# Splitting the token-shift transfer of the last stage into one of 112 rows and one of 15

## The reference, cut to what matters

```python
def shift_tokens(t):
    a, s = jnp.split(t, 2, -1)
    s = jnp.pad(s, ((0, 0), (1, 0), (0, 0)))[:, :-1]
    return jnp.concatenate([a, s], -1)

def ffn_layer(x, g, bln, W1, b1, W2, b2):
    mu = x.mean(-1, keepdims=True)
    var = ((x - mu) ** 2).mean(-1, keepdims=True)
    xn = (x - mu) / jnp.sqrt(var + 1e-05) * g + bln
    hg = xn @ W1 + b1
    a, gate = jnp.split(hg, 2, -1)
    return a * jax.nn.gelu(gate, approximate=False) @ W2 + b2

for i in range(DEPTH):                      # DEPTH = 6
    x = attn_layer(shift_tokens(x), Wqkv[i], q_scale[i], k_scale[i], Wo[i]) + x
    x = ffn_layer(shift_tokens(x), ln_g[i], ln_b[i], W1[i], b1[i], W2[i], b2[i]) + x
```

## Time and profile before

| | us |
|---|---|
| median of 3 runs | 4162.72 |
| lowest and highest of them | 4159.46, 4164.74 |
| the profiled execution, its own time | 4165.06 |
| its span, first to last instruction | 4163.3 |
| its mean granted TensorE clock | 0.974 |

### The profile page before, as it was taken

One profiled execution on the slowest core, in us unless ns is written; L12 is line 12 of the kernel. 1 busy time (PEld: TensorE's weight loads), 2 busy tenths in 40 slices (PEclk: granted clock), 3 DMA queues, 4 the chain that ended last, 5 costly groups with the idle time before them and its releaser, 6 DMA issues.

```text
span 4163.3 us, 97842 instructions
## 1 busy us (share of the span) xinstructions
PE 3871.8 (93%) x36632; PEld 2544.0 (61%) x36632; DVE 2904.2 (70%) x10275; ACT 2580.5 (62%) x6856; POOL 1243.2 (30%) x810
## 2 busy tenths in 40 slices
PE   8979578899988999999999999999999999999996
PEld 5668445566655666666666666666666666666664
DVE  3542357788868887777777777777777777777773
ACT  2213246667766767677776676777766766767662
POOL 1103300000005433343434434333434343434330
PEclk9979789999999999999999999999999999999998
DMA  6002210000011001111011101010011101111010
GB/s 181 23 21 73 66 60 2 7 19 22 9 42 29 22 22 48 32 32 27 18 49 30 43 17 53 26 36 24 23 48 32 37 22 38 33 40 29 17 37 18
DMA packets 110785, 146.33 MB, mean 35 GB/s; under 512 B 35748, under 2 KB 77200, under 8 KB 109936
## 3 DMA queue, kind: packets, MB, share of 16 engines
q1 hardware_dynamic: 106912, 130.76, 10.9%
q0 software_dynamic: 3408, 9.31, 0.9%
HBM read 78.31 MB, written 11.40 MB: 22 GB/s over the span
## 4 chain that ended last, share of the span: by engine, by line
PE 54%; DVE 9%; POOL 4%; issue 2%; DMA 1%; ACT 0%; SPq 0%; DVEq 0%; POOLq 0%
PE psum L489 17%; PE psum L586 9%; PE psum L469 7%; PE psum L570 6%; PE psum L603 5%; PE psum L549 4%; PE psum L523 4%; POOL f_rn L892 3%; DVE f_rot L710 2%; DVE f_prob L753 1%; DVE f_rot L712 1%; DVE f_ss L717 1%; DVE f_xn L807 1%; PE psum L592 1%; DVE f_prob L781 1%
## 5 line engine op out<-in xcount | busy, mean ns | idle before, releaser
L489 PE MATMUL psum<-f_wqkv,f_xsT 128*128 128x512 f32 x2304 | 1072.1, 595 | 4.3 <-ACT f_raw L636 2.6
L887 POOL TENSOR_TENSOR f_raw<-f_rot 128x512 f32<-128x512 f32 x384 | 488.7, 1273 | 1663.8 <-DVE f_rot L712 1663.8
L650 ACT ACTIVATE f_prob<-f_prob,f_nb,f_rq 128x128 f32<-128x128 f32 x1536 | 740.1, 487 | 38.6 <-DVE f_nb L766 37.7
L489 PEld LDWEIGHTS psum<-f_wqkv,f_xsT 128*128 128x128 f32 x2304 | 402.5, 191 | 334.2 <-issue 329.4
L892 POOL TENSOR_TENSOR f_rn<-f_ss,f_half_pow 128x32 f32<-128x32 f32 x96 | 524.4, 5463 | 11.2
L586 PE MATMUL psum<-f_xnT,f_w 128*128 128x512 f32 x960 | 437.9, 595 | 2.2 <-ACT f_hT L673 1.1
L753 DVE CUSTOM_DVE_ANT_0 f_prob<-psum,f_band 128x128 f32<-128x128 f32 x1536 | 352.8, 285 | 115.9 <-PE psum L523 114.7
L634 ACT ACTIVATE f_sq<-psum 128x512 f32<-128x512 f32 x384 | 227.8, 593 | 231.1 <-PE psum L489 231.0
L781 DVE TENSOR_SCALAR f_prob<-f_prob,f_rs 128x128 f32<-128x128 f32 x1536 | 341.2, 286 | 13.6
L570 PE MATMUL psum<-f_wo,f_oT 128*128 128x256 f32 x1536 | 347.4, 379 | 1.6 <-ACT f_v L636 0.9
L710 DVE TENSOR_TENSOR f_rot<-f_raw,f_tab 128x512 f32<-128x512 f32 x384 | 333.4, 868 | 14.3 <-DMA x_before_mlp<-x_all 14.3
(11 more groups left out here) (248 smaller groups left out, 6978.3 us busy)
## 6 DMA issues: line engine op xcount, KB each, us to landing
f_v_near<-f_v SPq DMA_DIRECT2D x168, 256.0 KB, 3.5
f_wqkv<-in_Wqkv SPq DMA_DIRECT2D x36, 512.0 KB, 5.8
w_moe_W<-in_L_ffn_W SPq DMA_DIRECT2D x2, 4096.0 KB, 22.4
f_w<-in_W SPq DMA_DIRECT2D x12, 640.0 KB
f_wo<-in_Wo SPq DMA_DIRECT2D x6, 1024.0 KB, 6.4
f_xs<-x_all SPq DMA_DIRECT2D x24, 254.0 KB
expert_rows<-m_y SPq DMA_DIRECT2D x39, 128.0 KB, 1.7
h_mask_int<-in_mask_BxSxS_ik SPq DMA_DIRECT2D x16, 256.0 KB, 2.6
```

The lines of the kernel that those rows point to most:

```text
L489: mm = nc.tensor.matmul(ps.ap(step), xsT[:, c, t * P:(t + 1) * P], wqkv[:, c, i * HALF:(i + 1) * HALF], start=c == 0, stop=c == KC - 1)
L650: ex = nc.scalar.activation(pr, pr, ACT.Exp, bias=nb[:, t % 2, h:h + 1], scale=rq8[:, t, h:h + 1], accum_out=sums[:, t % 2, h:h + 1])
L887: nc.gpsimd.tensor_tensor(raw[:, (4 * t + i) % 8, :], rot[:, n % 2, 0, :], rot[:, n % 2, 1, :], ALU.add).then_inc(rope_done, 1)
```

## The change

Partition rows 1 to 127 of `xs` are no longer filled by one transfer. `EVEN` is (128 - 1) // 16 * 16 = 112: one transfer fills partitions 1 to 112, a second one partitions 113 to 127. The transfer for partition 0 stays. Three transfers now count on `xs_ready` in each body, so VectorE waits for 48 per iteration in place of 32. Nothing else changes.

```diff
--- before.py
+++ after.py
@@ -175,6 +175,7 @@
     H, DH = 16, 64
     WINDOW = W = 64
     R = 32
+    EVEN = (P - 1) // 16 * 16
     TB = 4
     NB = x_all.shape[1] // TB
     KC = D // P
@@ -391,7 +392,8 @@
 
                 at = (b - 1) % NB * TB
                 wait_drained(sp, ps, ("wo", -1, TB - 1), it)
-                sp.dma_start(xs[1:P, :, :], x_all[0:P - 1, at:at + TB, P:D]).then_inc(xs_ready, 16)
+                sp.dma_start(xs[1:EVEN + 1, :, :], x_all[0:EVEN, at:at + TB, P:D]).then_inc(xs_ready, 16)
+                sp.dma_start(xs[EVEN + 1:P, :, :], x_all[EVEN:P - 1, at:at + TB, P:D]).then_inc(xs_ready, 16)
                 sp.dma_start(xs[0:1, 1:TB, :], x_all[P - 1:P, at:at + TB - 1, P:D]).then_inc(xs_ready, 16)
 
             def load_old(n):
@@ -787,7 +789,7 @@
                                                 ).then_inc(ps.sem_drained(step), 1)
                     elif kind == "ln":
                         f = it + off
-                        dve.wait_ge(xs_ready, (f + 1) * 32)
+                        dve.wait_ge(xs_ready, (f + 1) * 48)
                         for t in range(TB):
                             nc.vector.bn_stats(stat[:, t, 0:6], x_all[:, tile(f, t), 0:P])
                             ins = nc.vector.bn_stats(stat[:, t, 6:12], xs[:, t, :])
```

## The result

Twenty runs of the changed kernel have a median of 4155.49 us (4151.09 to 4162.15), twenty of the kernel before 4163.07 us (4155.13 to 4170.17). The ratio is 0.9983 with a 95% interval of 0.9977 to 0.9989: 0.17% faster, within the 0.2% that the prediction counted as no difference, and in the direction that it forecast. In microseconds the interval is 4.6 to 9.6. The profiled execution took 4154.31 us around a span of 4152.5 us.

The account below looks back on a forecast made before the run. Mid-stage bodies were taken as bound by TensorE, with the transfer exposed only in the last body. The median of 4162.72 less 7.15 us, all else at zero, gave 4155.6 us, 0.17% faster; range 4151.5 to 4160.0.

Parts of the forecast that it names:

- One wait, one place: VectorE waits for the shift transfer only before the last body's statistics, 7.2 us; the other 23 bodies hide it.
- One engine of 16: The 127-row transfer into xs is done by one DMA engine, read from a mean share of 0.07.
- The gain of 7.15 us: Last body: statistics start at 4102.34 in place of 4109.49, and the end moves by the full 7.15 us.
- The landing, 5.4 us with 4.2 as the lower end: Last body: split transfer lands at 4098.8, three issues of 0.76 plus 3.1 us after 4093.43; bounds 4097.6 to 4103.0.
- The added issue at zero: SP's queue, one more issue per body: costs nothing while the residual sum covers it, 0.76 us without that cover.
- The clock: TensorE in the last body: same half-clock stretch after a 10.3 us idle time, charged zero; bounds 3.5 us gain, 1.5 loss.
- The split does not spread: Rival, 7%: both pieces of the shift still go through one engine, with one issue more; time 4163.5 us.
- Denser writes hold TensorE: Rival, 3%: sixteen engines writing xs hold TensorE in every body, at worst 74 us in all, time 4230.
- The clock comes back sooner: Rival, 8%: TensorE's restart in the last body wins up to 3.5 us more, time 4152.1, faster by 0.26%.
- The earlier loads at zero: SP's queue is free about 10 us earlier in all 24 bodies; the loads behind it, started earlier, gain zero.

Follow-up runs that it names:

- e1: The kernel before with the split made in the last body alone, the other 23 bodies keeping the 127-row transfer; ratio 0.9981 to the kernel before.
- e2: The kernel before with the split made in the 23 ordinary bodies and not in the last; ratio 1.0001 to the kernel before.
- e5: e3 with the split one row further on, 113 and 14 rows; one run, statistics 14.39 us after the first issue, tail 67.9 us.
- e4: The kernel before, unsplit, with the last body's layer norm steps moved before the residual sum; ratio 0.9998 to the kernel before.
- e7: e3 with the last body's layer norm also before the second products' additions and the unshifted half's statistics before the wait; ratio 0.9968 to the kernel before.
- e12: e7 with the 112 rows cut into seven pieces of 16, nine issues in place of three; landing 7.29 us after the first issue, single run 4144.29 us.
- e3: The changed kernel with the last body's layer norm steps moved before the residual sum; ratio 0.9972 to the kernel before.
- e11: The version of e7 run once more, beside common runs of the kernel before; ratio 0.9970 to the kernel before, median 4150.45 us.
- e6: e3 with the split at 96 and 31 rows; one run, statistics 6.27 us after the first issue, behind a wait of 1.02 us.

## Why the prediction was right, step by step

**One wait, one place.** Right, and shown: the wait list named the transfer once, and e1 and e2 put the whole gain into that one body.

**One engine of 16.** Read from a DMA share of 0.07. e5 shows it from the other side: 113 rows behave like 127 and have the same share, 112 do not, and reach 0.76. The reading that "the queue cannot hand it on while the first transfer's pieces are being drained" is right in kind, but the hold ends 2.9 us before the drain does (e4).

**The gain of 7.15 us.** Measured 7.28 in the profiles, and 7.6 between the medians of twenty runs, whose interval only says 4.6 to 9.6. From the first issue to L794 I had counted 8.91 us (4102.34 - 4093.43) and it was 8.78: L794 reads nothing that the last instruction of the sum writes, and it starts at 4099.35, before L858 is over at 4099.44, and not 0.04 us behind it. The sum of 4155.6 us stands beside a median of 4155.49; with runs that scatter over 11 us, agreement to 0.1 us is luck, agreement to 1 or 2 us is not.

**The landing, 5.4 us with 4.2 as the lower end.** Too high: 3.46 (e7), below the lower bound. The term that was mis-sized is "a landing of 2.8 to 5.3" set behind three whole issues. It was taken from copies of 256 KB. Of the three pieces the one of that size, 112 rows or 224 KB, is issued first, and it is there within 3.46 us of its own issue; behind the start of the last issue, of 1.5 KB, only 1.8 us passed. It cost nothing, since the sum covered anything up to 8.8 us.

**The added issue at zero.** Right under that cover. Uncovered it costs 0.64 us (e12), where I had written 0.76.

**The clock.** It fell and stayed low as assumed, for 1.15 us less after resuming, so that the first 24 products behind the transposes took 12.44 us in place of 13.02. Charging nothing for it was right: from TensorE's resumption to the end the fourteen traces have 47.0 to 48.1 us, with no order by the length of the pause. But the reason I gave ("still twice the 5.0 us after which the clock fell here") is not sound: the table below has a fall 1.8 us after TensorE stopped. It would have misled me for a pause of 4 us.

**The rivals.** "The split does not spread" is refuted by e7 for 112 and 15 (3.46 us in place of 16.06), and is true of the 113 rows of e5. The advice of the Trainium skill that stood beside it (DMA: Bandwidth & Descriptors, Rules for kernel authors), not to cut a transfer by partitions, did not hold for this one of 127 rows. For halves that divide well no run here tests it; the nearest is e12, where cutting the 112 rows further cost 3.83 us. "Denser writes hold TensorE" is refuted by bodies of 118.47 us. "The clock comes back sooner" did not happen as an outcome of its own: in this profile it came 1.15 us sooner, which is most of the 0.66 us, but in e1, with the same pause, it took 8.4 us.

**The earlier loads at zero.** Right: e2 is worth nothing, and the queue now waits 2226.3 us for ScalarE before the copies of `v`, where it was 2092.1 in the earlier trace rows. The time that it was held has become time that it waits.

The wait of SP's queue in the changed kernel (us in total, times, longest):

```profile
SPq L387 <- ACT f_v L638: 2226.3, 96, 34.3
```

## What to carry to other kernels

When a transfer takes many times what its bytes should, look at the share of the 16 DMA engines while it runs: 0.07 was one of them here. Then try a cut whose large piece has a multiple of 16 rows (112 and 96 were fast here, 127 and 113 slow), and give each added issue 0.6 to 0.9 us of the queue. One row more or less can decide. Before counting the gain, find each place that waits for the transfer: here 23 of 24 were hidden, and what the transfer then uncovered (the order of the steps in the last body) was worth another 3.5 us of the tail, of which e4 had at most 1.5 without the split.

## What the runs showed that I had not expected

**The clock falls after short pauses too.** Before the transposes of the last body TensorE stood still for different times in these kernels. From stretches of a quarter of a microsecond, the time from its stop to the fall of the granted clock to half, and from its resumption to the return to full:

| | pause us | fall after stop us | full again after resuming us |
|---|---|---|---|
| before | 17.47 | 5.0 | 8.1 |
| after | 10.17 | 3.4 | 6.9 |
| e3 | 6.56 | 3.4 | 7.1 |
| e7 | 3.85 | 1.8 | 8.2 |
| e11, the same kernel as e7 | 3.85 | 3.3 | 6.2 |

e7 and e11 are the same kernel with the same pause. The stretches around e7's pause, columns as in the earlier trace rows:

```profile
4094.06:4095.86 1.80, 0.00 (x1) 0.00 (x0) 0.65 (x6) 0.00 (x0) 1.01 (x1) 1.00 0.00 0
4095.88:4097.90 2.02, 0.00 (x0) 0.00 (x0) 2.02 (x9) 0.00 (x0) 0.00 (x0) 0.50 0.00 0
4097.91:4106.10 8.19, 7.12 (x14) 3.76 (x15) 5.17 (x16) 3.52 (x4) 1.01 (x1) 0.50 0.27 86
```

and e11's:

```profile
4093.98:4097.26 3.28, 0.00 (x1) 0.00 (x0) 2.12 (x12) 0.00 (x0) 1.01 (x1) 1.00 0.00 0
4097.27:4104.08 6.81, 5.17 (x12) 3.08 (x13) 5.25 (x17) 2.84 (x3) 1.01 (x1) 0.50 0.22 77
```

e7 spent 10.2 us at half clock, e11 6.8. So shortening the pause from 17.5 to 3.9 us never kept the clock up. Over all fourteen traces the fall comes 1.8 to 5.0 us after the stop and the full clock 6.2 to 8.4 us after the resumption, neither in step with the pause. The whole half-clock stretch is steadier: 20.5 us in all five traces with a pause of 15.6 to 17.6 us, 13.7 in all three with 10.2 us, 10.2 in all four with 6.6 to 7.7 us, and differs only in the two with 3.85 us. A shorter pause thus shortened the time at half clock mostly by the part in which TensorE stood still anyway. What sets the moment of the fall these runs don't show.

**Spans differ upstream of everything that changed.** The first shift is issued between 1382.2 us (e12) and 1395.3 us (e6) in these profiles, 13 us apart, before any edited instruction of the stage has run. For a change worth 7 us a difference of two single spans is no measure; a length between two events of the trace is.
